# A two-layer perceiver block on one core: 89 matmuls whose result nothing reads are taken out

## The reference, cut to what matters

```python
x = x + L0_xattn(x, ctx)      # 16 heads of 16, quantised q, k, v and weights
x = x + L0_attn(ln(x))        # 16 heads, difference of two softmaxes, causal
x = x + L0_ffn(ln(x))         # 8 small experts, 2 per token, and a shared one
x = x + L1_xattn(ln(x), ctx)  # 16 heads of 128, rms-normed q and k
x = x + L1_attn(ln(x))        # latent attention with rotary positions
x = x + L1_ffn(ln(x))         # 8 experts of 704, 2 per token, tokens gathered
```

## Time and profile before

| | us |
|---|---|
| median of 3 runs (lowest, highest) | 792.55 (789.72, 794.78) |
| the profiled execution | 789.43 |
| its span, first to last instruction | 787.6 |
| PE busy | 727.2 (92%) |
| DVE busy | 569.0 (72%) |
| ACT busy | 409.1 (52%) |
| POOL busy | 235.7 (30%) |
| mean granted TensorE clock | 0.91 of full |

### The profile page before, as it was taken

The page is one execution under the profiler, slowest core; times in us unless marked ns, Lnnn a source line. Parts: engine busy times, 40 slices in busy tenths (PEclk is TensorE's granted clock), DMA queues, the critical chain, the costliest instruction groups (busy, mean ns, idle before and its releaser), DMA issues.

```text
span 787.6 us, 15787 instructions
## 1 busy us (share of the span) xinstructions
PE 727.2 (92%) x5914; PEld 576.8 (73%) x5914; DVE 569.0 (72%) x903; ACT 409.1 (52%) x890; POOL 235.7 (30%) x286
## 2 busy tenths in 40 slices
PE   8889998899999988989998799998979998999997
PEld 6633333678888867877876589986758886899997
DVE  6999997578888856787989566654568856766654
ACT  2878888335444434534454666664235552344442
POOL 3032111413233225442457022222134320322211
PEclk8955555799999999999999999999889999999999
DMA  6099999202221122311122011112011163999994
GB/s 196 27 153 169 174 170 180 68 14 75 81 62 42 34 61 82 99 49 46 47 61 61 7 37 32 54 28 87 14 42 43 40 213 130 335 344 341 343 339 150
DMA packets 131210, 89.24 MB, mean 113 GB/s; under 512 B 80225, under 2 KB 114273, under 8 KB 131138
## 3 DMA queue, kind: packets, MB, share of 16 engines
q1 hardware_dynamic: 129842, 84.74, 40.6%
q0 software_dynamic: 1296, 3.54, 1.4%
HBM read 65.05 MB, written 6.42 MB: 91 GB/s over the span
## 4 chain that ended last, share of the span: by engine, by line
PE 56%; DVE 18%; issue 11%; ACT 6%; POOL 4%; DMA 3%; SPq 1%; DVEq 1%; POOLq 0%; ACTq 0%
PE ps L205 10%; PE ps L207 9%; PE ps L206 9%; PE ps L2454 8%; PE ps L1722 4%; DVE x L1489 2%; PE ps L2104 2%; PE ps L1702 2%; POOL nb L874 2%; DVE qrot L2277 2%; PE ps L1192 2%; PE ps L1203 1%; ACT soft L2238 1%; PE ps L687 1%; DVE hh L1479 1%
## 5 line engine op out<-in xcount | busy, mean ns | idle before, releaser
L337 POOL TENSOR_TENSOR wa_lo<-raw,wa_hi 128x256 fp32r<-128x256 f32 (+1 forms) x76 | 86.8, 1147 | 188.2 <-ACT wa_hi L326 187.8
L337 POOL TENSOR_TENSOR wb_lo<-raw,wb_hi 128x256 fp32r<-128x256 f32 (+1 forms) x68 | 61.3, 906 | 128.3 <-ACT wb_hi L326 128.3
L967 ACT ACTIVATE kres<-ps,nb,qs 128x1024 int16<-128x1024 f32 x64 | 76.9, 1203 | 16.9 <-POOL nb L874 12.3
L1096 DVE TENSOR_REDUCE nm<-ps 128x1 f32<-128x1024 f32 x64 | 77.3, 1221 | 7.4 <-PE ps L803 5.6
L803 PE MATMUL ps<-qkt 48*128 48x512 bf16 x128 | 64.4, 605 | 6.7 <-ACT kres L967 5.8
L205 PE MATMUL ps<-xt_hi,wa_hi 128*128 128x512 f32 (+1 forms) x168 | 68.8, 409 | 1.6 <-DVE soft L1347 0.9
L2454 PE MATMUL ps<-xgt,tw 128*128 128x128 f32 x600 | 69.7, 275 | 0.5 <-ACT xgt L2550 0.5
L2454 PEld LDWEIGHTS ps<-xgt,tw 128*128 128x128 f32 x600 | 68.3, 192 | 0.8 <-ACT xgt L2550 0.7
L206 PE MATMUL ps<-xt_lo,wa_hi 128*128 128x512 f32 (+1 forms) x168 | 64.9, 386 | 0.0
L207 PE MATMUL ps<-xt_hi,wa_lo 128*128 128x512 f32 (+1 forms) x168 | 64.8, 386 | 0.0
L205 PE MATMUL ps<-wb_hi,ot_hi 128*128 128x256 f32 x192 | 57.1, 297 | 1.6 <-DVE ot_lo L2282 0.9
(11 more groups left out here) (441 smaller groups left out, 1886.5 us busy)
## 6 DMA issues: line engine op xcount, KB each, us to landing
tw<-w_l1f SPq DMA_DIRECT2D x15, 1280.0 KB, 7.7
tw<-w_l1f SPq DMA_DIRECT2D x15, 640.0 KB, 8.2
raw<-w_l0a SPq DMA_DIRECT2D x16, 256.0 KB, 2.9
raw<-w_l1p SPq DMA_DIRECT2D x32, 128.0 KB, 2.1
raw<-w_l1x SPq DMA_DIRECT2D x32, 128.0 KB, 2.1
raw<-w_l1a SPq DMA_DIRECT2D x16, 256.0 KB, 2.6
tw<-w_l1f SPq DMA_DIRECT2D x60, 64.0 KB, 7.7
raw<-w_l0f SPq DMA_DIRECT2D x12, 256.0 KB, 2.7
```

Of the source, the lines that this page charges most:

```text
L337: last = nc.gpsimd.tensor_tensor(split_lo, src, split_hi.bitcast(F32), ALU.subtract)
L967: nc.scalar.activation(ei[:, n % RING, :], slot(n), ACT.Exp, bias=nb[:, n % 3:n % 3 + 1], scale=qs[:, col:col + 1], accum_out=sums[:, u, k ...
L1096: nc.vector.tensor_reduce(nm[:, n % 3:n % 3 + 1], slot(n), AX.X, ALU.max, negate=True).then_inc(x0["nm"], 1)
```

## The change

Every call of `busy` goes, and with them the function and the argument `idle` of `ln_pe`. Nothing else is changed: no other instruction, wait, semaphore or order. TensorE issues 89 matmuls of 128x512 bfloat16 and their 89 weight loads less.

```diff
-        def busy(pe, bank, count):
-
-            for _ in range(count):
-                nc.tensor.matmul(ps[:, bank, :], ident_bf[:], ident_bf[:].unsqueeze(1).broadcast_to([P, 4, P]), start=True, stop=True)
-
-        def ln_pe(pe, n, base=0, idle=None):
+        def ln_pe(pe, n, base=0):
             for t in range(NT):
                 if t % 2 == 0:
-                    if idle is not None:
-                        busy(pe, idle[0], idle[1 + t // 2])
                     pe.wait_ge(ln_xn, 2 * n + t // 2 + 1)
...
-            if idle is not None:
-                busy(pe, idle[0], idle[3])
...
             l0x_turn_out(pe, 1)
-            busy(pe, 5, 3)
             l0x_out(pe, 1, range(NT))
...
-            ln_pe(pe, 1, 2, idle=(5, 7, 0, 2))
+            ln_pe(pe, 1, 2)
...
-            ln_pe(pe, 2, 4, idle=(2, 10, 2, 2))
+            ln_pe(pe, 2, 4)
...
                 some(out_x, 2 * n, 0)
-                if n == -2:
-                    busy(pe, 4, 10)
                 some(turn_x, 2 * n + 4, 0)
                 if within(2 * n + 2):
                     mix_ctx(pe, n + 1, 1)
-                if n == -2:
-                    busy(pe, 4, 3)
                 some(key_scores, 2 * n + 6, 0)
...
             l1a_tables(pe)
-            busy(pe, 3, 2)
             pe.wait_ge(x_ready, 8)
             y_start(R_PB)
-            ln_pe(pe, 4, idle=(3, 0, 2, 2))
+            ln_pe(pe, 4)
...
             last.then_inc(la["lt"], 1)
-            busy(pe, 2, 4)
             pe.wait_ge(la["lte"], 2)
...
-                if j == 0:
-                    busy(pe, 2, 6)
                 if j == STEPS - 1:
                     l1a_out(pe, j - 1, 0, 0)
-                    busy(pe, 2, 3)
                 l1a_turn(pe, j, j % 2)
...
-            ln_pe(pe, 5, 4, idle=(2, 10, 2, 2))
+            ln_pe(pe, 5, 4)
...
             last.then_inc(mo["logits"], 1)
-            busy(pe, 2, 8)
...
-            busy(pe, 2, 8)
 
             pe.wait_ge(mo["first_at"], mo_at("first_at", 1))
...
-            busy(pe, 2, 1)
             for m in range(TILES + 1):
```

## The result

| | before | changed |
|---|---|---|
| median of 4 runs each, us | 791.64 (789.72 to 794.78) | 801.65 (800.22 to 804.59) |
| ratio, 95% interval | | 1.0155 [1.0121, 1.019] |
| profiled execution, us | 789.43 | 804.59 |
| its time at the low clock, us | 143.8 in 9 stretches | 190.8 in 12 |
| its mean granted clock | 0.910 | 0.882 |

The changed kernel is slower by 10 to 12 us. The profile after comes from the slowest of its four runs, and that of before from an execution faster than all four timed: of the 15.2 us between the two, 3 to 5 are the luck of the draw.

A forecast was written before the change was run, and what follows sets the result against it. TensorE's granted clock was taken to matter, with dummies holding it through waits. Losses of 10.0 us less 2.6 won made +7.4 us, added to the 792.55 median: 800.0 us, range 791 to 810.

The forecast's parts named there:

- Two effects and no third: All 89 dummies: they take time on TensorE's queue and are work it shows while otherwise standing still; nobody waits for them.
- Gain of 2.6 us, half of what stands in the chain at low: Dummies in the chain of waits: removal gives back 2.3 us at low, half counted, and 0.3 us at high.
- End of the first cross attention, +0.6: Without the 3 dummies at 142.58 the clock stays low for the output matmuls: 0.6 us lost, bounds 0 and 1.1.
- Layer norms of L0, 0.5 and 0.9, net 1.1 with the first step: Before L0 attention and L0 ffn: the clock falls earlier, 0.5 and 0.9 us lost, from between 0 and 1.7.
- L1 cross attention, +1.4, net 0.8: Start of the heads, 10 and 3 dummies: a low clock there costs 1.4 us, bounds 0 and 1.7; net 0.8.
- the third rival: The clock stays low for long, as in the first cross attention, over L1 attention steps: 812 to 832 us, chance 0.09.
- L1 attention, +3.3, net 2.1: First step's scores and projection matmuls go low, possibly twice: 3.3 us lost, bounds 0 and 8; net 2.1.
- The nearest row: L1 attention at 581.2, same pattern without dummies: scores took 3.68 instead of 2.08; taken to say the first step goes low.
- L1 ffn up to the gather, +3.3: Transposes, gate, ranks, token and place products run low without 31 dummies: 3.3 us lost, bounds 0.9 faster to 5 slower.
- The first rival: The dummies cost more than they hold, so removal is faster: 789 or 786.3 us, chance 0.09.
- The second: Rival: the clock costs little altogether, gains and losses cancel, within 3 us of 792.6; chance 0.22.
- the trace's signs: Low windows behind 563.9 and between 659 and 669, gate about 3 us, first scores 3.7, mean clock 0.89 to 0.90.

## Why the prediction was right, and where it was not

800.0 was forecast, 801.65 and 800.08 were measured; 1.0093 by the forecast against 1.0155 and 1.0137. Direction, range and mechanism held; the change was too small, 7.4 us against 10.0 by the medians and 10.8 to 12.3 by the ratios. That 800.0 nevertheless lies so near is luck: two errors cancel. The forecast called 789.43 a lucky execution and started from 792.55, the median of three runs; 59 later runs of the kernel before, on three chips, have medians of 789.4 to 790.3, so the start was 2 to 3 us too high. By its own steps:

- *Two effects and no third.* Shown by the run with one-row dummies: without work in the array they only cost.
- *Gain of 2.6 us, half of what stands in the chain at low.* Too large. The 3 at 438.38 (1.28 us in the chain) stood over ACT's copy `ptx`, which the scores wait for in any case; without them the scores start 1.89 us behind the transposes' start, with them 2.0 to 2.4 where the clock is low, so 0.1 to 0.5 us was to be had and not 0.64. The chain of waits names the last releaser, and a dummy that ends a little later than the real one hides it.
- *End of the first cross attention, +0.6.* Right in size and mechanism. The long low stretch ends at 143.0 to 145.7 in the seven traces that keep its 3 dummies, at 147.6 to 156.7 in the five without. The output product of the changed kernel is low throughout (window 144.0 to 147.4 at 0.50), and the deltas at its last matmul and at the next transposes are +1.1 and +0.7 against those before it.
- *Layer norms of L0, 0.5 and 0.9, net 1.1 with the first step.* The first execution lost 5.28 before the heads, the second 0.03; the averages of five traces without and four with dummies differ by 2.6. For the whole step chance is as large as the effect, and it stays open. Its parts are clearer: 141 to 157 loses 1.3 us on average with the first step (0.7 forecast, net), 281 to 300, the second layer norm, nothing that can be seen (-0.8 to 0.4 without its dummies, -1.6 to 0.0 with them; 0.5 forecast, net).
- *L1 cross attention, +1.4, net 0.8.* **This step was mis-sized**: 4.1 us by six traces (5.0 by the whole column, with the late transfer at the heads' end), 4 to 6 by the run with only this place out. I took the price of one short low stretch, 3.2 us long as at 151.1, as the upper bound (1.7). It lasted 13.7 us, because the work behind the wait is small products with waits of 0.7 to 2.1 us between them, and behind them it did not come back sooner. The first cross attention's 106 us had shown that work can go on at low for long, and I used it only for the third rival. There too the reading was off: it blamed matmuls of 16 columns, which take 22.7 us of that stretch. Most of it is another product, of 512 columns and only 48 of 128 rows (view by lines of the kernel before, 38 to 144 us):

```profile
L803 PE MATMUL ps<-qkt 48*128 48x512 bf16 x122 | 62.7, 616 | 6.2 <-ACT kres L967 5.8
```

That fits the run with the one-row dummies, which have 512 columns and few rows too; no run changed this stage. At the L1 cross attention the wait is the same with 3 dummies behind it and without (4.68 and 4.70 us idle), and the stretch is 6.8 or 13.7 us long: what follows the wait decides how long it lasts.
- *L1 attention, +3.3, net 2.1.* The difference of averages is 2.1, but with a spread of 5 us. The place where I expected it, the first step's scores, went high in the first trace of the changed kernel (2.08 at 577.48), and the second step's went low (3.37); in the second trace both are low (3.58, 3.68), as forecast. The nearest row was less near than it seemed: the scores at 576.12 are the second step's, behind the 6 dummies, and those at 585.89 the third's; the first's start at 566.52.
- *L1 ffn up to the gather, +3.3.* Right: 3.5 in both traces of the changed kernel, 3.6 as a difference of averages. The gate took 3.11 in the chain (3.0 forecast), the token products 3.78 (3.6). Two smaller terms were wrong and cancel: the first transposes stayed at high (0.66 in both traces; +0.44 forecast), and the two pairs gave back 0.4 instead of 0.9.

The first rival (dummies cost more than they hold) fell with the run that takes out those in the chain. The second fell by the ratio's interval; and the Trainium skill's rule behind it ("TensorE: Matmul & The Clock Gate", section "What's actually happening"), that ramping costs under 1% of a typical kernel's span, does not hold for this kernel: 1.4 to 1.6%, on top of what the kernel before still pays. The third did not come to pass as one long stretch in the L1 attention; its mechanism came in two other places at a smaller size. Of the trace's signs these were there: the gate near 3 us, low windows behind the last layer norm, more low time in all. The first step's scores at 3.7 came in one trace of two. Dips that begin in the wait came at the heads in both and at the second L0 layer norm in one; at the last layer norm the dip began 1.8 and 1.5 us behind the wait. The mean clock fell further, to 0.882 and 0.884 instead of 0.89.

Over 149 runs (4 of the changed kernel, 86 of the experiments' kernels without the one-row kernel, 59 of the kernel before), the time at low worked out from each run's span and mean clock goes with its span at 0.23 us of span for each us at low, correlation 0.93. Work at low takes up to twice its time (0.43 for 0.23) and would cost up to 0.5 if all of it were waited for, so by this estimate about half the time at low costs nothing.

## What to carry to other kernels

Where TensorE waits, price the wait by what comes after it: where dense matmuls followed, the clock was back after 3.4 us (151.0 in the kernel before) and filling the wait is worth little; where small products with waits followed, 3 dummies that join up with the first real work saved more than 10 that end early. Before trusting "idle time of an engine costs nothing", look at the granted clock of the next stretch. When executions of one kernel differ by 5 us, compare traces by the differences between matched instructions, place by place: four ratios within 0.1% of each other held four different stories.

## What the runs showed of the hardware

- Matmuls over one row with 512 columns, among the same real work, keep TensorE busy (16.57 of 17.0 us at 673.9) and leave the granted clock at 0.50, where full 128-row ones of the same length hold it at 1.00 (4.00 of 4.0 us at 658.0).
- In the changed kernel and its repeat the two long low stretches have the same lengths, 13.7 and 17.1 us, though they begin at different instants; the first is 13.7 us in all six traces without the dummies of its place, the second 13.7, 17.1 and 20.5 in the other three without its own. The stretches that come and go between the changed kernel's two traces are 3.4 to 6.8 us.
- Products with only 8 columns slow at low like any other: 16 of the gate's take 3.22 us instead of 1.85.
